# Sampled-softmax loss: x transposed two tiles at a time, bias in two transposes, no dummy products, earlier label gathers

## What is computed

```python
inputs = front_emb[movie_id[:, 0]]
true_w = after_emb[labels];        true_b = after_bias[labels]
samp_w = after_emb[sampled_ids];   samp_b = after_bias[sampled_ids]
true_logits = jnp.sum(inputs * true_w, axis=-1) + true_b
sampled_logits = jnp.einsum('bd,sd->bs', inputs, samp_w) + samp_b
...
hits = sampled_ids[None, :] == labels[:, None]
sampled_logits = jnp.where(hits, sampled_logits + NEG_INF, sampled_logits)
logits = jnp.concatenate([true_logits[:, None], sampled_logits], axis=1)
loss = jax.nn.logsumexp(logits, axis=1) - logits[:, 0]
```

## Time and profile before

| | |
|---|---|
| median of 3 runs | 59.97 us (59.93 to 60.43) |
| profiled execution, time on the device | 59.7 us |
| its span in the profile | 57.9 us |
| VectorE busy | 48.2 us (83%) |
| ScalarE busy | 42.7 us (74%) |
| GpSimd busy | 38.8 us (67%), 40 gathers |
| TensorE busy | 33.8 us (58%) |

### The profile page before, as it was taken

How to read it: one execution, slowest core, us unless ns; L and a number is a source line. 1 busy time by engine, 2 the same in 40 slices (tenths; PEclk the granted TensorE clock), 3 DMA queues, 4 the chain that set the end, 5 groups by cost and what they waited for, 6 DMA issues and landing times.

```text
span 57.9 us, 608 instructions
## 1 busy us (share of the span) xinstructions
PE 33.8 (58%) x137; PEld 23.1 (40%) x137; DVE 48.2 (83%) x134; ACT 42.7 (74%) x70; POOL 38.8 (67%) x48
## 2 busy tenths in 40 slices
PE   0000083999939929996999699929918992000000
PEld 0000051826517708853777467707707770000000
DVE  2699888876879999999999958997999999995230
ACT  4303999688987759899998999489878789950020
POOL 4067677777667777767777767777766777776000
PEclk9999999999999999999999999999999999997555
DMA  0482222232010111100111001011011011110100
GB/s 0 161 198 63 46 46 46 66 68 54 23 23 23 31 35 24 23 23 23 23 43 26 23 23 40 23 36 33 23 23 23 23 32 36 24 23 23 23 0 6
DMA packets 1715, 2.17 MB, mean 38 GB/s; under 512 B 944, under 2 KB 944, under 8 KB 1712
## 3 DMA queue, kind: packets, MB, share of 16 engines
q0 software_dynamic: 1280, 1.59, 12.1%
q1 hardware_dynamic: 432, 0.55, 3.5%
HBM read 2.13 MB, written 0.01 MB: 37 GB/s over the span
## 4 chain that ended last, share of the span: by engine, by line
POOL 28%; DVE 26%; issue 14%; DMA 12%; ACT 9%; PE 5%; POOLq 2%; DVEq 0%
POOL w_rows L228 13%; POOL t_rows L228 13%; DVE psum L515 12%; DVE masks L407 9%; ACT psum L346 6%; DMA x_rows<-front,rows 4%; DMA t_rows<-after,rows 4%; DMA id_cols<-ids 3%; DVE xT L427 2%; POOLq L62 2%; ACT masks L328 2%; PE psum L297 2%; POOL x_rows L228 2%; PE psum L299 1%; PE psum L298 1%
## 5 line engine op out<-in xcount | busy, mean ns | idle before, releaser
L515 DVE CUSTOM_DVE_ANT_0 psum<-psum,masks 128x1024 f32<-128x1024 f32 x16 | 19.4, 1232 | 0.0
L346 ACT ACTIVATE psum<-psum,lowest 128x1024 f32<-128x1024 f32 x16 | 17.3, 1080 | 2.7 <-DVE lowest L515 2.7
L228 POOL DMA_INDIRECT x_rows<-front,rows x16 | 15.1, 945 | 4.9 <-issue 4.6
L228 POOL DMA_INDIRECT t_rows<-after,rows x16 | 15.1, 943 | 4.9 <-issue 4.3
L297 PE MATMUL psum<-wT_high,xT 128*128 128x512 f32 x32 | 13.5, 420 | 4.9 <-ACT psum L346 3.8
L299 PE MATMUL psum<-b_parts,ones 128*128 128x512 f32 x32 | 12.7, 396 | 0.0
L298 PE MATMUL psum<-wT_low,xT 128*128 128x512 f32 x32 | 12.6, 394 | 0.0
L228 POOL DMA_INDIRECT w_rows<-after_twice,rows x8 | 7.7, 967 | 4.0 <-issue 2.1
L407 DVE TENSOR_SCALAR_CACHE_REDUCE masks<-sample_f,label 128x1024 f32<-128x1024 f32 x8 | 10.2, 1277 | 0.2
L297 PEld LDWEIGHTS psum<-wT_high,xT 128*128 128x128 f32 x32 | 6.0, 187 | 8.6 <-issue 5.1
L328 ACT ACTIVATE masks<-sample_ids,neg_label 128x1024 f32<-128x1024 int32 x8 | 9.1, 1139 | 0.0
(11 more groups left out here) (80 smaller groups left out, 33.6 us busy)
## 6 DMA issues: line engine op xcount, KB each, us to landing
sample_ids<-sample_row SPq DMA_DIRECT2D x1, 512.0 KB, 4.1
x_rows<-front,rows POOLq DMA_INDIRECT x16, 2.4
t_rows<-after,rows POOLq DMA_INDIRECT x16, 2.4
w_rows<-after_twice,rows POOLq DMA_INDIRECT x8, 2.6
id_cols<-ids SPq DMA_DIRECT2D x1, 20.0 KB, 1.8
out<-loss SPq DMA_DIRECT2D x1, 8.0 KB, 1.4
```

What stands on the lines that cost most here:

```text
L228: return pool.indirect_dma_start(dst, None, table, bass.IndirectOffsetOnAxis(ap=rows[:, col:col + 1], axis=0))
L346: nc.scalar.activation(logits(t), logits(t), ACT.Exp, bias=lowest[:, t:t + 1], scale=-1.0, accum_out=sums[:, t:t + 1]).then_inc(exp_ok, 1)
L515: V.tensor_tensor_reduce(out=logits(t), in0=logits(t), in1=masks[:, t, :], scale=1.0 / SHRINK, scalar=3e38, op0=ALU.add, op1=ALU.min, accu ...
```

## The change

- x rows of an even and an odd tile now lie next to each other in `x_rows` (even tiles with the constant 1 in front, odd tiles behind), and one transpose of 128x128 turns both; the even tile comes out in rows 0 to 63 of the bank, the odd one in 64 to 127. `raise_x` and `lower_x` work tile by tile, on 128 columns; an odd tile has its high half in rows 64 to 127 of `xT`. A score waits for its own tile.
- Label rows of even tiles come from a second table, `before`, with the bias in front, to fit this layout.
- The bias goes through two transposes, of 128x12 and 128x4. Row 2j and 2j + 1 of the result belong to sample tile j; ScalarE writes each tile's 128 columns with all rows at once, times a factor per row (`own`) that is 0 for the rows of other tiles: six copies and two instead of one and one. VectorE makes `own` by two small instructions ahead of `split_b`.
- The nine `keep_busy` products are gone.
- The last four label gathers wait for 13 scores; before, tile 12 waited for 14, tile 14 for 15 and tile 15 for 16.

```diff
-SCORED_BEHIND_LABELS = (7, 8, 8, 9, 9, 10, 11, 11, 11, 12, 13, 13, 14, 14, 15, 16)
+SCORED_BEHIND_LABELS = (7, 8, 8, 9, 9, 10, 11, 11, 11, 12, 13, 13, 13, 13, 13, 13)
...
+        def x_high(t):
+
+            return slice(EMBED, TWICE) if t >= 2 and t % 2 else slice(0, EMBED)
...
+        def x_of(a, b):
+
+            return x_rows[:, a:b, :].rearrange("p t n -> p (t n)")[:, 1 - a % 2:1 - a % 2 + (b - a) * EMBED]
...
                     elif t == 2:
-                        pool.wait_ge(b_turned, 3)
+                        pool.wait_ge(b_turned, 1)
...
-                    gather(t_rows[:, t, :], after, LAB + t).then_inc(t_in[k], 16)
+                    gather(t_rows[:, t, :], (before, after)[t % 2], LAB + t).then_inc(t_in[k], 16)
...
+            def turn_b(k):
+
+                pe.wait_ge(b_split_ok, k + 1)
+                first, last = B_TILES[k]
+                nc.tensor.transpose(psum[0:2 * (last - first), 4 + k, 0:P],
+                                    b_split[:, first:last, :].rearrange("p j h -> p (j h)").bitcast(f32), ident[:, :]
+                                    ).then_inc(b_turned, 1)
...
                 if g >= 2:
-                    pe.wait_ge(xT_ok, g - 1)
-                for i, t in enumerate(range(*X_GROUPS[g])):
-                    m = nc.tensor.transpose(psum[0:EMBED, x_bank(g), i * P:(i + 1) * P], x_rows[:, t, 0:EMBED],
-                                            ident[:, :])
-                m.then_inc(x_turned, 1)
-
-            def keep_busy(n):
-                for _ in range(n):
-                    nc.tensor.matmul(psum[:, 7, :], ones[:, :], ones[:, 0:1].to_broadcast([P, BANK]),
-                                     start=True, stop=True)
+                    pe.wait_ge(xT_ok, X_GROUPS[g - 2][1])
+                a, b = X_GROUPS[g]
+                nc.tensor.transpose(psum[0:(b - a) * EMBED, x_bank(g), 0:P], x_of(a, b), ident[:, :]).then_inc(x_turned, 1)
...
-                        pe.wait_ge((b_low_ok, b_high_ok)[h], 1)
+                        pe.wait_ge(b_parts_ok, (h + 1) * SAMPLE_TILES // 2)
...
+            def spread_b(k):
+
+                act.wait_ge(b_turned, k + 1)
+                first, last = B_TILES[k]
+                n = 2 * (last - first)
+                for j in range(first, last):
+                    nc.scalar.mul(b_parts[B_AT[k]:B_AT[k] + n, j * P:(j + 1) * P], psum[0:n, 4 + k, 0:P],
+                                  own[0:n, j - first:j - first + 1]).then_inc(b_parts_ok, 1)
+
             def raise_x(g):
                 act.wait_ge(x_turned, g + 1)
-                n = x_cols(g).stop - x_cols(g).start
-                nc.scalar.mul(xT[0:EMBED, x_cols(g)], psum[0:EMBED, x_bank(g), 0:n], -SHRINK).then_inc(x_high_ok, 1)
+                for t in range(*X_GROUPS[g]):
+                    nc.scalar.mul(xT[x_high(t), tile_cols(t)], psum[x_high(t), x_bank(g), 0:P], -SHRINK
+                                  ).then_inc(x_high_ok, 1)
...
             def lower_x(g):
-                dve.wait_ge(x_high_ok, g + 1)
-                n = x_cols(g).stop - x_cols(g).start
-                V.scalar_tensor_tensor(xT[EMBED:, x_cols(g)], psum[0:EMBED, x_bank(g), 0:n], -SHRINK,
-                                       xT[0:EMBED, x_cols(g)].bitcast(f32), ALU.mult, ALU.subtract).then_inc(xT_ok, 1)
+                for t in range(*X_GROUPS[g]):
+                    dve.wait_ge(x_high_ok, t + 1)
+                    V.scalar_tensor_tensor(xT[x_low(t), tile_cols(t)], psum[x_high(t), x_bank(g), 0:P], -SHRINK,
+                                           xT[x_high(t), tile_cols(t)].bitcast(f32), ALU.mult, ALU.subtract
+                                           ).then_inc(xT_ok, 1)
...
+            dve.wait_ge(ident_ok, 1)
+            link(V.tensor_reduce(own_pair[:, :], ident[0:2 * SAMPLE_TILES, 0:2 * SAMPLE_TILES].rearrange(
+                "p (j h) -> p j h", h=2), mybir.AxisListType.X, ALU.add))
+            V.tensor_scalar(own[:, :], own_pair[:, :], SHRINK, None, ALU.mult).then_inc(own_ok, 1)
             dve.wait_ge(log_count_ok, 1)
```

More of the change, by code:

```diff
@@ L19 @@
 SLOTS = 3
+B_TILES = ((0, 6), (6, 8))
+B_AT = (0, 32)
 QUARTERS = 4
@@ L41, with log_uniform_loss @@
 LN2_LOW, LN2_HIGH = -0.00021219444, 0.6933594
-def log_uniform_loss(nc, ids, sample_row, front, after, after_twice, out):
+def log_uniform_loss(nc, ids, sample_row, front, before, after, after_twice, out):
     f32, f32r, i32 = mybir.dt.float32, mybir.dt.float32r, mybir.dt.int32
@@ L574 @@
         "front": got["L0_rec_front_emb"],
-        "after": np.concatenate([got["L0_rec_after_emb"], got["L0_rec_after_bias"].reshape(VOCAB, 1)], axis=1),
-    }
-    arrays["after_twice"] = np.concatenate([got["L0_rec_after_emb"], arrays["after"]], axis=1)
-    for k in ("front", "after", "after_twice"):
+        "before": np.concatenate([bias, after], axis=1),
+        "after": np.concatenate([after, bias], axis=1),
+        "after_twice": np.concatenate([after, after, bias], axis=1),
+    }
+    for k in ("front", "before", "after", "after_twice"):
         arrays[k] = np.concatenate([arrays[k], np.repeat(arrays[k][-1:], SPREAD, axis=0)])
```

46 lines of the change are left out of this document (19 added, 27 removed).

## The result

The changed kernel takes 62.45 us (median of 4 runs, 62.23 to 63.1), the one before, run beside it, 59.95 (4 runs, 59.56 to 60.43): a ratio of 1.043 [1.032, 1.054]. Slower was the likelier sign in the forecast, but its +0.8 us and its range of 59.8 to 61.9 are missed. The profiled execution took 62.66, its span is 60.6 where it was 57.9.

The account below looks back on a forecast made before the run. GpSimd's back-to-back gathers were taken as the floor, VectorE close behind with 1.73 us of slack. Lateness 2.34 + 0.15 = 2.49 less 1.73 gave +0.8 on 59.97, so 60.8 us; range 59.8 to 61.9.

Parts of the forecast that it names:

- Gathers as the floor: GpSimd: 40 gathers stand back to back, 1.248 us each, never waiting for a score; the diff shortens none.
- gaps over 0.3: Sign of being wrong, between GpSimd's gathers: a score is late and the end moves one for one with it.
- Slack of 1.73: VectorE's tail: it may come 1.73 us later before the end moves, since its last dot product waits for label rows.
- Score 0 at 17.94: TensorE's first score starts 0.51 us later, behind bias copies on ScalarE stepping 0.22 and then lower_x(0).
- Eleven products slow: TensorE without dummies: 11 of the 12 products of tiles 0 and 1 step 0.43 us; bounds 6 and 18.
- turn_x(2) to reduce 1: From the transpose at 22.90 through raise and lowers (0.42 a pair) to VectorE's reduce 1 at 23.95, 2.34 us late.
- x two tiles at a time: Raises on ScalarE, lowers on VectorE: 0.07 us more per pair; six pairs +0.15, bounds -0.3 to +0.8.
- rival 2: TensorE's slow level lasts through tile 2, 18 slow products: 3.3 + 0.15 - 1.73 = +1.7, 61.7 us; chance 0.12.
- Sum: VectorE at reduce 15: 2.34 + 0.15 = 2.49 us late, less the slack of 1.73: +0.76, called +0.8 us.
- Hidden: Rival: nine or fewer products slow, the tail's slack holds nearly all; no change within 0.6 us, 60.0; chance 0.38.
- The slow level lasts through tile 2: The same as rival 2: 18 slow products on TensorE, 61.7 us; chance 0.12.
- Faster: Rival: GpSimd's waits cost the 0.3 ahead of gathers; three removed save 0.9 us, 59.1; chance 0.04.

Follow-up runs that it names:

- before_x_split: The kernel before with each pair's raise and lower cut into two 64x128 instructions on the same partitions (rows 0 to 63): 70.41 us beside 70.41, on a chip with standstills.
- no_dummies_3: The kernel before without its nine dummy products, on a chip without standstills: 59.95 us beside 59.72, ratio 1.004 [1.0026, 1.0055].
- after_dummies_4: The changed kernel with the nine dummy products back: 61.92 us beside 59.81, ratio 1.034 [1.027, 1.040].

## Why the prediction was right and wrong

- **Gathers as the floor:** this held for the kernel before and fell for the changed one. In the changed kernel four gathers waited 0.16 to 0.48 us longer for scores, and the last comes 1.09 late. The forecast took gaps over 0.3 as a sign that the end moves one for one with them. It did not: with its gather 1.09 late the last dot product could have started at 54.87 + 1.09 = 55.96, and VectorE reached it at 57.52. The last four gathers stand 0.30 apart, so their changed waits are worth 0 in this trace, as forecast.
- **Slack of 1.73:** right to 0.01. Reduce 15 late less last dot late is 3.20 - 1.46 = 1.74, 4.32 - 2.58 = 1.74, 4.39 - 2.65 = 1.74, and the 1.45 and 0.88 of the kernels under it leave 0.05 and 0.18.
- **Score 0 at 17.94:** came at 18.04. The bias copies step 0.25 where 0.22 was taken, and square 5 starts at 15.83 (15.7).
- **Eleven products slow:** twelve in this trace, and the first of them steps 0.59. With the late start, turn_x(2) stands at 23.32 where 22.90 was forecast. The middle of 6 and 18 was a guess, and that it came within one is luck: three other traces with the same early work on TensorE have six, seven and twelve.
- **turn_x(2) to reduce 1:** 1.05 was forecast, 24.72 - 23.32 = 1.40 is measured. The slow transpose and the raise's start took 0.46 instead of 0.33, the pair of lowers 0.64 instead of 0.42. With the point above, reduce 1 is 0.77 later than the 23.95 of the sum.
- **The step that failed: "x two tiles at a time".** It took 0.07 more for each pair, twice the step between overlapping instructions, which `before_x_split` shows right for two instructions on the same partitions. The change moves the second to the other half, where nothing overlapped. On VectorE the pair lets the next start after 0.64 instead of 0.35, so 0.29 more, on ScalarE after 0.59 instead of 0.27. Six pairs at 0.29 are 1.7, of which 1.28 remained at reduce 15 (0.15 forecast). Its bound was wrong as well: "no overlap, 2 x 0.28 - 0.42" takes the instruction's duration off, when what counted before was its step of 0.35; 2 x 0.28 - 0.35 = 0.21 for each pair is up to +1.3 for six (0.29 was measured, since short gaps stand between them too). With that the forecast's own case reaches 59.97 + 2.34 + 1.3 - 1.73 = 61.9 and rival 2 reaches 62.8, and the range should have gone past 62.
- **Sum:** 4.39 late instead of 2.49, 1.90 too little: 0.77 + 1.13. With the first pair's 0.64 - 0.42 = 0.22 out of the 0.77, the pairs carry 1.35 of it; later scores carry 0.42 and the slower way from transpose to raise 0.13. Less the slack, 2.65 at the last dot product, 2.5 in the medians.
- **Rivals.** *Hidden* fell: with twelve slow the start alone is over the slack. It is what `no_dummies_3` shows for the dummies alone, four to five slow and +0.2 us. *The slow level lasts through tile 2* fell: score 2's first steps are 0.34 and then 0.23. *Faster* fell: no gap of GpSimd got shorter than 0.30.
- The Trainium skill (TensorE: Matmul & The Clock Gate, Part 1: The HAM clock gate) puts the ramp's penalty under 1% of a typical kernel's span. In this kernel it is 12 x 0.20 = 2.4 of 62 us, near 4%; that the engine begins throttled and activity raises it agrees with the dummies' 0.43 at the start and the fast scores behind them.

What stays open: what decides when TensorE's level rises (19.5 to 23.3 here), so how much of the loss the bias transposes and how much chance carries; the price of the clock alone in the changed kernel; the 0.2 us of `no_dummies_3`. The new bias path alone and the changed kernel without its pairs ran only on chips with standstills, so neither has a time that counts. On the chips without them no kernel tried beats the one before; in those that come within 0.2 us of it the last dot product still waits for its gather.

## What to carry to other kernels

Count what the next instruction waits (the step from one start to the next), not durations, and where one instruction becomes two on different partition halves, or its neighbours lie on other rows, assume that nothing of them overlaps until a row shows it (0.64 against 0.40 here). First work out the slack of the later engine against the floor, since two changes that each fit into it can together exceed it: here pairs alone (1.45) and missing dummies alone (0.88) cost 0.0 and 0.2 us, and all together, with the bias path, 2.5. Where a term depends on when the clock rises, give it a range of its own, and don't judge a change by the number of slow products in one trace.

## What the runs showed of the hardware that was not expected

**The granted clock can read 1.00 where TensorE runs at half of it.** In the changed kernel the column reads 1.00 in the stretch from 18.0 to 23.3 with twelve products 0.43 apart; in `after_dummies_4`, where the column had changed by 17.3, it reads 0.50 there. The changed kernel's page, PEclk in 40 slices of 1.5 us (9 is 90% or more), where slices 13 to 15 hold the slow products:

```profile
PEclk9999999999999999999999999999999999999955
```

In these traces, ahead of the column's first change only the distances between products tell the level.

**Standstills on some chips.** The kernel before, without any edit, run as an experiment of its own on such a chip:

> The kernel before, unchanged, for its trace on the chip of this call. Theory (the eight to ten microseconds more that it took beside the experiments so far are spells in which all engines stand still together): the trace has two or three such spells of 1 to 3 us, near the first scores and ahead of reduce 15, and otherwise the durations and steps of the first trace (gathers 1.25 us apart, reduces 1.23). Rival (everything runs slower on those chips): the steps themselves are longer.

70.60 us beside 70.62 for the same kernel. Its waits (us in total, times, longest), put down to "remote":

```profile
ACT wT_high L337 <- remote: 4.5, 1, 4.5
...
DVE psum L515 <- remote: 3.0, 1, 3.0
...
POOL x_rows L228 <- remote: 2.5, 1, 2.5
```

The windows ahead of the first standstill and in it (columns as above):

```profile
16.00:18.00 2.00, 1.12 (x6) 0.32 (x5) 0.35 (x2) 0.16 (x1) 1.50 (x2) 1.00 0.13 32
...
19.50:21.50 2.00, 0.00 (x0) 0.00 (x0) 0.42 (x1) 0.85 (x3) 0.58 (x1) 0.50 0.00 0
```

From 19.5 to 21.5 TensorE does nothing and DMA moves 0 GB/s; the little that VectorE, ScalarE and GpSimd do (0.42, 0.85 and 0.58) starts at 20.65. ScalarE waited 4.49 us ahead of its next instruction at 20.65; then all goes on with the steps of the other chips (a gather 1.25, products 0.43 and then 0.23 to 0.24). Against the first trace of this kernel its reduces fall 5.0 us back by reduce 0, 2.4 more at reduce 4 and 3.1 more at reduce 15; so three such stretches make most of the 10 us. Score 0 then runs at 1.2 GHz in the kernel with its dummies too, which is why the dummies can't be judged there. What halts the core is open; nothing in the kernels differs between the chips.
